# VectorE's program of an edge group rewritten, and slot marks moved from ScalarE to VectorE, in a one-core graph layer

## What is computed

```python
msgs = edge_val[:, None] * xn[edge_col]
agg = segment_sum(msgs, edge_row, 3125)           # edges are not sorted within what the kernel may assume
gnn = agg @ W.T + b
msg = linear_attention(xn)                        # q, k, v, 8 heads, elu + 1
msg = layernorm(msg @ Wm, g1, b1)
h = relu(concatenate([xn, msg]) @ W1) @ W2
x = x + gnn + xn + layernorm(h, g2, b2)
p = softmax(layernorm(x) @ gate_w + gate_b); keep the top 2 of 16, renormalised
x = x + sum over the two experts of (silu(n3 @ w1) * (n3 @ w2)) @ w3 * share
```

## Time and profile before

| | us |
|---|---|
| median of three runs (lowest, highest) | 1327.99 (1327.07, 1331.26) |
| span of the profiled execution, first to last instruction | 1249.4 |
| groups 0 to 12, by the profile | 119.9 to 782.0 |
| experts and the end | from 860 on |

### The profile page before, as it was taken

The page is one execution under the profiler, slowest core; times in us unless marked ns, Lnnn a source line. Parts: engine busy times, 40 slices in busy tenths (PEclk is TensorE's granted clock), DMA queues, the critical chain, the costliest instruction groups (busy, mean ns, idle before and its releaser), DMA issues.

```text
span 1249.4 us, 21035 instructions
## 1 busy us (share of the span) xinstructions
PE 1089.0 (87%) x6272; PEld 933.1 (75%) x6272; DVE 800.6 (64%) x1896; ACT 675.8 (54%) x1630; POOL 610.4 (49%) x625
## 2 busy tenths in 40 slices
PE   6797789999999999989999998716999999999990
PEld 5675677777777777767777787306999999999980
DVE  7875678888888888888888877673222222222226
ACT  4568697898978979789797874311011011011000
POOL 5937556575675766757557570002333333333320
PEclk9898899999999999999999999767999999999995
DMA  7214222232222322223223230325999999999958
GB/s 221 87 35 123 68 72 81 72 93 77 85 85 72 93 74 84 89 71 92 76 81 89 75 102 7 103 95 176 335 325 334 331 335 330 330 334 333 335 170 307
DMA packets 113487, 196.08 MB, mean 157 GB/s; under 512 B 13506, under 2 KB 61440, under 8 KB 113408
## 3 DMA queue, kind: packets, MB, share of 16 engines
q1 hardware_dynamic: 84073, 120.62, 28.8%
q0 software_dynamic: 26112, 71.34, 18.2%
q10 hardware_dynamic: 3222, 3.20, 0.7%
HBM read 177.12 MB, written 17.99 MB: 156 GB/s over the span
## 4 chain that ended last, share of the span: by engine, by line
PE 48%; DVE 14%; ACT 14%; issue 6%; DVEq 6%; POOL 6%; DMA 3%; ACTq 3%; SPq 0%; POOLq 0%
PE psum L1058 19%; PE psum L1068 9%; PE psum L964 7%; ACT in_slot L413 6%; POOL arena L702 5%; PE psum L973 3%; DVE agg L1319 2%; ACT first_use L427 2%; PE psum L895 2%; DMA arena<-y_rows,gather_i 2%; DVE agg L1325 2%; PE psum L885 2%; DVE agg L1700 1%; ACTq L414 1%; ACT arena L530 1%
## 5 line engine op out<-in xcount | busy, mean ns | idle before, releaser
L702 POOL DMA_INDIRECT arena<-y_rows,gather_i x416 | 437.5, 1052 | 250.9 <-PE psum L964 78.2
L964 PE MATMUL psum<-arena,hot 128*128 128x256 f32 x832 | 218.3, 393 | 14.9 <-issue 6.5
L635 ACT ACTIVATE arena<-psum 128x512 f32<-128x512 f32 x64 | 38.2, 597 | 327.6 <-PE psum L1058 327.6
L1319 DVE TENSOR_TENSOR agg<-psum,agg 128x256 f32 x416 | 174.6, 420 | 55.1 <-DVE agg L1319 31.0
L964 PEld LDWEIGHTS psum<-arena,hot 128*128 128x128 f32 x832 | 151.3, 192 | 49.7 <-issue 26.8
L1058 PEld LDWEIGHTS psum<-arena 128*128 128x128 f32 x1536 | 181.2, 194 | 4.9 <-issue 2.5
L530 ACT ACTIVATE arena<-arena,listed 128x256 f32<-128x256 f32 x416 | 172.6, 495 | 21.7 <-DMA arena<-y_rows,gather_i 21.7
L1058 PE MATMUL psum<-arena 128*128 128x128 f32 x1536 | 181.7, 277 | 2.0 <-DVE arena L1657 2.0
L973 PE MATMUL psum<-arena,first_use 128*128 x624 | 161.0, 394 | 25.2 <-ACT first_use L429 24.8
L1664 DVE TENSOR_TENSOR arena<-psum,arena 128x512 f32<-128x512 f32 x64 | 44.2, 691 | 204.8 <-PE psum L1058 204.8
L718 POOL DMA_INDIRECT chosen_rows<-arena,back_at x64 | 63.3, 988 | 219.7 <-DVE arena L1671 215.0
(11 more groups left out here) (227 smaller groups left out, 1634.7 us busy)
## 6 DMA issues: line engine op xcount, KB each, us to landing
arena<-in_L_ffn_w_dram SPq DMA_DIRECT2D x144, 512.0 KB, 5.8
xnT<-in_L_ffn_w_dram SPq DMA_DIRECT2D x48, 512.0 KB
arena<-y_rows,gather_i POOLq DMA_INDIRECT x416, 2.8
arena<-chosen_rows SPq DMA_DIRECT2D x4, 1280.0 KB, 9.9
y_rows<-w ACTq DMA_DIRECT2D x6, 512.0 KB, 2.9
agg<-in_x_dram SPq DMA_DIRECT2D x4, 640.0 KB, 6.6
n_rows<-arena SPq DMA_DIRECT2D x4, 640.0 KB
out_dram<-agg SPq DMA_DIRECT2D x4, 640.0 KB
```

What stands on the lines that cost most here:

```text
L702: pool.indirect_dma_start(rows[h][:, t, :], None, y_rows, bass.IndirectOffsetOnAxis(ap=gather_i[h][:, t:t + 1], axis=0)).then_inc(gathered ...
L964: pe.matmul(bank_of(g, t // 2)[:, (t % 2) * C:(t % 2 + 1) * C], hot[:, (g * GT + t) % HOTS, :], rows[h][:, t, :], start=True, stop=True).t ...
L1319: dve.tensor_tensor(own, bank_of(g, t // 2)[:, (t % 2) * C:(t % 2 + 1) * C], own, ALU.add).then_inc(evicted, 1)
```

## The change

In words, then the core of the diff.

- VectorE makes the slot marks (`mark_slots`), as one comparison of 128x1024 bf16 elements; `in_slot` has pairs of columns innermost. `place_f` goes; `place_b` holds tile and slot. ScalarE's `slot_hot` goes.
- In groups 1 to 12 the drains inside the steps go. Operations that depend on each other are two steps apart or more, with an addition that waits for the one before it between them. Drains stay in `first_root`, in two places in groups 9 and 10, in group 0 (`beside_first`) and ahead of the groups.
- `mark_bins` and `count_marks` of group g+3 stand in the cross phase of group g (steps 30, 33), and the prefix of g+2 at step 0; the sort of g+2 runs through steps 0 to 26, its reorders at 20, 24, 29, 32, and its list is done at step 55, a group earlier than before.
- `first_root` moves from step 7 to 15 on VectorE, the turn of n1 from 15 to 19 on TensorE, merge from 5 to 7, the turn of the message from 1 to 3, the hidden layer to 22, 23, 25, 28, attend from 49 to 40.
- The one-hot batches of rows 8, 16 and 24 are made at steps 2, 8 and 18, and that of the next group's row 0 at step 28. The bin numbers are loaded at step 33, behind the scan.
- All three batches of cross one-hots have a place of their own, and ScalarE's order is rewritten.

```diff
+            def mark_slots(g, k):
+                if g * CHUNKS + k >= 2:
+                    dve.wait_ge(reordered, g * CHUNKS + k - 1)
+                whole = [P, CH // 2, P, 2]
+                two = place_b[:, 1, k * CH:(k + 1) * CH].rearrange("p (a b) -> p a b", b=2)
+                dve.tensor_tensor(in_slot[k % 2][:, :, :, :], two.unsqueeze(2).to_broadcast(whole), slot_no[:, :, :].unsqueeze(1).to_broadcast(whole),
+                                  ALU.is_equal).then_inc(slot_hot_ready, 1)
...
-                    last = pe.matmul(in_order, in_slot[k % 2][:, c, :], record[k % 2][:, c // 2, :, :, c % 2].rearrange("p f t -> p (f t)"),
+                    last = pe.matmul(in_order, in_slot[k % 2][:, c // 2, :, c % 2], record[k % 2][:, c // 2, :, :, c % 2].rearrange("p f t -> p (f t)"),
...
             def beside(g, step):      # TensorE, groups 1 to 12
+                if step == 0 and sorts:
+                    prefix(g + 2)
+                if step == 3:
                     turn_tok(g, d_msg, d_msgT)
                 if step == 4 and more:
                     turn_list(g + 1)
+                if step == 7:
                     merge(g)
+                if step == 9 and more:
                     pick_list(g + 1)
+                if step == 19:
                     turn_tok(g, d_n1, d_n1T)
+                if step == 22:
                     hidden(g, 0)
+                if step == 23:
                     hidden(g, 1)
+                if step == 25:
                     hidden(g, 2)
+                if step == 26 and more:
                     query(g + 1)
+                if step == 28:
                     hidden(g, 3)
+                if step in (20, 24, 29, 32) and sorts:
+                    reorder(g + 2, (20, 24, 29, 32).index(step))
...
             def beside(g, step):      # VectorE, groups 1 to 12
+                sorts, more, counts = g + 2 < NG, g + 1 < NG, g + 3 < NG
+                if step == 0 and sorts:
+                    add_prefix(g + 2)
+                if step == 2 and sorts:
+                    mask_places(g + 2)
+                if step == 4 and sorts:
+                    sum_places(g + 2)
+                if step == 6 and sorts:
+                    split_places(g + 2)
+                if step == 8 and sorts:
+                    keep_places(g + 2)
+                if step == 9:
                     pair_stats(0, g, d_merged, 5)
+                if step in (10, 14, 19, 23) and sorts:
+                    mark_tiles(g + 2, (10, 14, 19, 23).index(step))
+                if step == 11:
                     pair_moments(0, g)
                 if step == 11 and more:
                     keep_picked(g + 1)
+                if step in (12, 16, 21, 25) and sorts:
+                    make_record(g + 2, (12, 16, 21, 25).index(step))
+                if step in (13, 18, 22, 26) and sorts:
+                    mark_slots(g + 2, (13, 18, 22, 26).index(step))
+                if step == 15:
+                    first_root(g)
+                if step == 28 and more:
+                    hot_batch(g + 1, 0)
+                if step == 30 and counts:
+                    mark_bins(g + 3)
+                if step == 33 and counts:
+                    count_marks(g + 3)
...
+                if step == 55 and sorts:
+                    mark_starts(g + 2)
...
# ScalarE, groups 1 to 12
+                    message_turned(g)
+                    if more:
+                        keep_list(g + 1)
                     scale_rows(g, 7)
+                    cross_hot(g, 0)
                     std(0, g)
+                    if more:
+                        scale_rows(g + 1, 0)
                     first_scaled(g)
+                    if more:
+                        scale_rows(g + 1, 1)
                     n1_turned(g)
+                    cross_hot(g, 1)
+                    hidden_relu(g, 0)
...
```

More of the change, by code:

```diff
@@ L907, in down, with beside_first @@
                     last.then_inc(d_down, 1)
+            def beside_first(step):
+                if step == 3:
+                    attend(0)
+                if step == 4:
+                    turn_list(1)
+                if step == 9:
+                    turn_tok(0, d_msg, d_msgT)
+                if step == 12:
+                    merge(0)
+                if step == 13:
+                    pick_list(1)
+                if step == 19:
+                    turn_tok(0, d_n1, d_n1T)
+                if step == 20:
+                    prefix(2)
+                if step == 21:
+                    hidden(0, 0)
+                if step == 22:
+                    hidden(0, 2)
+                if step == 23:
+                    hidden(0, 1)
+                if step == 25:
+                    query(1)
+                if step == 29:
+                    hidden(0, 3)
+                if step == 34:
+                    down(0, 0)
+                if step == 35:
+                    down(0, 1)
+                if step == 49:
+                    attend(1)
+                if step in (33, 40, 46, 54):
+                    reorder(2, (33, 40, 46, 54).index(step))
             def beside(g, step):
                 sorts, more = g + 2 < NG, g + 1 < NG
-                if g == 0 and step == 3:
-                    attend(0)
-                if step == (9 if g == 0 else 1):
+                if step == 0 and sorts:
+                    prefix(g + 2)
+                if step == 3:
                     turn_tok(g, d_msg, d_msgT)
@@ L940, in beside @@
                     down(g, 1)
-                if step == 40 and sorts:
-                    reorder(g + 2, 1)
-                if step == 46 and sorts:
-                    reorder(g + 2, 2)
-                if step == 49 and more:
+                if step == 40 and more:
                     attend(g + 1)
-                if step == 54 and sorts:
-                    reorder(g + 2, 3)
             def add_up(g):
@@ L1469, in beside @@
-                if step == 50 and more:
-                    message_sums(g + 1)
-                if step == 51 and more:
+                if step == 43 and sorts:
+                    place_list(g + 2)
+                if step == 43 and more:
+                    message_sums(g + 1)
+                if step == 45:
+                    centre(g, 0)
+                    pair_root(1, g)
+                if step == 47 and sorts:
+                    clip_starts(g + 2)
+                if step == 47 and more:
+                    message_shares(g + 1)
@@ new lines, in beside @@
+                if step == 47:
+                    centre(g, 1)
+                if step in (49, 51):
+                    meets_pair = 2 * g + (step - 49) // 2 in range(step - 32, step - 28)
+                    if meets_pair:
+                        dve.drain()
+                    add_dense(g, (step - 49) // 2)
+                    if meets_pair:
+                        dve.drain()
+                if step == 51 and sorts:
+                    drop_whole(g + 2)
+                if step == 53 and more:
@@ L1490, in add_up @@
                         evict_pair(g, (step - GT) // 2)
-                    beside(g, step)
-                    if g + 1 < NG and step == 34:
+                    if g == 0:
+                        beside_first(step)
+                    else:
+                        beside(g, step)
+                    if g + 1 < NG and step == GT + 1:
                         its_bin = bins_named(g + 1)
```

362 lines of the change are left out of this document (189 added, 173 removed).

## The result

| | before | changed | ratio (95%) |
|---|---|---|---|
| the study of the result | 1328.32 | 1336.95 (1334.81 to 1340.19) | 1.007 [1.0045, 1.0094] |
| second study | 1327.15 | 1336.84 | 1.007 [1.0042, 1.0091] |
| third study | 1318.71 | 1335.35 | 1.013 [1.0087, 1.0169] |
| fourth study | 1250.76 | 1283.17 | 1.025 [1.0236, 1.027] |

Slower, and inside the range. How much slower depends on something that the prediction did not know: the same kernel before is timed at either of two levels, 1251 or 1319 to 1328 us, always at the same one within a study. The profile that the prediction read (span 1249.4) is of the lower level, the times it was scaled to are of the upper. I call them the lower and the upper level; kernels are compared only within one.

What follows compares the result with a forecast made beforehand. VectorE's program was taken to bound a sorting group, then a cycle through VectorE and TensorE. Groups +5, clock +12, start -3, group 0 +1 and end +2 make +17, so 1345 us, range 1302 to 1370.

Steps and rivals of the forecast that it cites:

- The bound and the cycle: Sorting groups: the four-step lead ties VectorE's first steps and TensorE's rest into one cycle, 52.3 us against 51.8.
- The clock: Behind the turn of n1: a hole drops TensorE's clock onto the hidden layer, 1.2 us a group, bounds 0 and 2.3.
- The scaling: Around the profiled span of 1249.4 us: 78.6 us up to the median of 1328.0 were taken to stay.
- the forecast of +17: Whole kernel: ten groups +5, clock +12, start -3, group 0 +1, end +2, together +17 us.
- A: Sorting groups: the four-step lead is covered and VectorE's shorter program decides, 48.5 us a group, 1290 us; chance 0.20.
- B: Sorting groups: the cycle as worked out, but the clock stays up or falls where TensorE waits anyhow, 1333 us; chance 0.22.
- C: TensorE's reorders: the weight load with a step costs its full 3.5 us a group, 1380 us; chance 0.07.
- D: VectorE's steps: dropping the drains gives nothing, since the engine holds the next operation anyway, 1357 us; chance 0.07.
- The wait at L865 (then L876) over 3 us: TensorE's wait for ScalarE's first_scaled, at 3 us or more a group, was to show the forecast.
- A clock of 0.5 behind the turn: On TensorE, a granted clock of 0.5 right after the turn of n1 was to show the forecast.
- Ten groups at 526 to 545: The ten sorting groups together at 526 to 545 us were to show the forecast.
- VectorE idle behind the cross matmuls: VectorE idle by some 5 us behind the cross matmuls in each group was to show the forecast.

Runs made afterwards that it cites:

- e11: The changed kernel with 28 unneeded transposes on TensorE ahead of the turn of n1, at the lower level: 1257.48 us, 1.0055 of before.
- e8: The changed kernel with 28 unneeded transposes on TensorE ahead of the turn of n1, at the upper level: 1313.41 us, 0.9965 of before.
- e1: The kernel before, unchanged, profiled again at the lower level: 1251.03 us, span 1249.3.
- e6: The kernel before, unchanged, in the third study, at the upper level: 1318.23 us, span 1316.5.
- e7: The changed kernel, unchanged, in the third study, at the upper level: 1335.35 us.
- e10b: The changed kernel, unchanged, in the fourth study, at the lower level: 1283.17 us, 1.025 of before.
- e12: The changed kernel with VectorE's first norm and ScalarE's std, first_scaled and n1_turned early, at the lower level: 1239.82 us, 0.991 of before.
- e3: The changed kernel with drains put back in 22 steps of each group, at the lower level: 1307.22 us, 1.045 of before.
- e5: The changed kernel with VectorE's first norm and ScalarE's std, first_scaled and n1_turned early, at the upper level: 1304.16 us, 0.981 of before.
- e4: The changed kernel, unchanged, in the second study, at the upper level: 1336.84 us, 1.007 of before.

## Why the prediction was right, and where it was off

**The bound and the cycle: right.** The prediction said that shrinking the lead from eight steps to four ties VectorE's steps 0 to 15 and TensorE's steps 19 to 55 into one cycle. In group 6 VectorE's first addition (461.77) stands 2.6 us behind TensorE's first row matmul (459.21), where 1.7 + 0.35 and a tail of 0.95 were worked out, 3.0. Steps 0 to 15 take 15.8, worked out 15.9; first_root to the turn (478.68) 1.1, as read. From the turn to the next group, with the clock kept up (e11, 464.81 to 497.50), it is 32.7, worked out 32.3. Together 52.2 against 52.3. The slot mark took 0.68 (0.69 said); the hole at the turn was 3.8 (3.9 said).

**The clock: the step that was mis-sized.** The mechanism is shown (e8, e11), the size was half. One stretch of 3.4 us at the low clock, in seven groups of ten, 1.2 us a group, was taken, with 2.3 as the upper bound. It is two stretches, in nine of the ten groups (one in group 10), and 4.9 us of needed work lie in them: 2.5 a group, past the bound. The prediction read the rate of one stretch in six groups of the kernel before, in which the hole was another one. By the timeline the turn's hole does not stand alone either: TensorE also waits 1.1 and 0.4 us for the ring of results just ahead of it.

**Terms that were not in the sum.** In group 1 TensorE waits 3.8 us at the prefix that the change put at step 0 (the group takes 59.7 instead of 54.7):

```profile
PE psum L733 <- DVE node_in_bin L1239: 3.8, 1, 3.8
```

The change also gave the prefix, from group 3 on, a wait for the list of the group ahead of it (`pe.wait_ge(list_kept, g)`), which the excerpt of the diff doesn't show. VectorE keeps the list of group 2 at the end of its group 0, behind most of the cross additions: L1239 ends at 184.48, TensorE's prefix starts at 184.63. The count of marks, which the prefix needs as well, was done at 178.4. Group 11, which sorts nothing, loses 6.7: TensorE waits there 3.2 us at the turn as well, and its clock falls. Ten groups: 10 x 0.4 of cycle, 10 x 2.5 of clock and 5 of group 1 make the 34; e11 splits it the same way, 527.7 - 518.2 = 9.5 with the clock up and 552.2 - 527.7 = 24.5 of clock.

**The scaling: wrong.** The step "what lies around it, 78.6, is taken to stay" rested on nothing: e1 and e6 show 1.7 us around the span at both levels. At the lower level, the one that was read, the forecast of +17 (1.3%) stands against +32.4. At the upper level, the kernel before itself takes 563 us for ten groups instead of 518, the changed one 582 instead of 552; of 34 us lost 19 are left, and group 11 loses nothing (51.7 and 50.5). So 1345 came near 1337 because two misses, a clock too cheap and a change of level that takes half of the loss back, offset each other: the direction and the cycle were foreseen, the nearness of the number was luck. Why the changed order suffers less from the upper level, the waits of e6 and e7 tell in the main. The kernel before loses 41.8 us at add_prefix, where VectorE stands until the prefix's increment arrives. The changed kernel makes the prefix at step 0; in its ten groups at the upper level (e7) VectorE has no wait at add_prefix (L1154), and all its waits together are 136 us instead of 107 (e10b), about the 30 us by which the ten groups are longer than at the lower level. No run moves the prefix alone, so this rests on the traces' waits.

One comparison of the prediction doesn't hold as written: four steps of TensorE, 1.7 us, are more than first_scaled's 1.1. They are less only than the 1.1 and one long operation of VectorE (1.08 for a record) together.

**The rivals.** A, that the shorter program of VectorE decides, was false for this order, and came partly true once the chain was out of the way: e12's groups of 50.2 are 1.6 shorter than before's 51.8, not the 3.3 of the rival. B, the cycle without a cost of the clock, is what e11 is: 1257.5, 1.0055, where B said +5. The changed kernel isn't that. C is false: the strided load takes 0.097 us in the median of 416 in e10b, where the contiguous one took 0.096. The mean of 0.107 in the row of L745 above holds loads at half clock, up to 0.145; in e11 and e12, where the clock stays up, none takes over 0.101. D is false by e3. The Trainium skill's "VectorE: DVE Perf Modes", section "The DRAIN you can't avoid", says that leaving out the semaphores between chained operations saves nothing, and also that an operation that is not held starts earlier; the prediction told only the first. As a rule that fewer fences save nothing it does not hold here: eight drains made the same sixteen steps 1.5 us longer.

**What was to show it.** The wait at L865 (then L876) over 3 us: yes. A clock of 0.5 behind the turn: yes. Ten groups at 526 to 545: no, 552. VectorE idle behind the cross matmuls: the wrong place; its 8.3 us are in rows behind the turn, the cross additions wait 1.3.

## What to carry to other kernels

An engine's program can be made denser and the kernel slower, as here, where the steps that were moved took the lead of a chain from eight steps to four. Before such a trade, add up the way from one meeting of the two engines to the next (52.3 here) as well as each engine's total (46.8 and 44.4), and take the larger. The hole of TensorE cost its wait and then 2.5 us of half-rate work behind it, so move the chain that ends it (e5: three steps of VectorE and three calls of ScalarE earlier, 43 us at the lower level), and if it can't be moved, matmuls into a bank about to be overwritten buy back the second part (26 us). Before a profile's span is scaled to timed runs, check that both are of the same level: a profiled run's own time beside its span does it.

## What the runs showed of the hardware

- The same program on one core ran at 1251 or at 1319 to 1328 us. At the upper level engines wait for increments of TensorE's semaphores long after the matmul (6.4 us at the prefix in group 5 of e6, 41.8 us of VectorE's time in ten groups), and the trace lacks records of increments (632 of 728 in e6); DMA traffic is the same 196 MB. One and the same chip stood at the upper level in e4 and e5 and at the lower in e10b. What sets the level stays open.
- 28 transposes of 128x128 fp32 took 3.22 us in a hole, and the 6.8 us at half clock behind it were gone.
